# A graph kernel of three edge passes: order of the preamble's steps, and a maximum taken first in the edge pass

## What is computed

```python
def _gat(x, src, dst, W, att_src, att_dst, bias, n):
    xw = (x @ W).reshape(n, H, D)
    a_src = jnp.einsum('nhc,hc->nh', xw, att_src)
    a_dst = jnp.einsum('nhc,hc->nh', xw, att_dst)
    logits = jax.nn.leaky_relu(a_src[src] + a_dst[dst], NEG_SLOPE)
    m = jax.ops.segment_max(logits, dst, num_segments=n)
    ex = jnp.exp(logits - m[dst])
    s = jax.ops.segment_sum(ex, dst, num_segments=n)
    out = jax.ops.segment_sum(xw[src] * (ex / (s[dst] + EPS))[..., None], dst, num_segments=n)
    return out.mean(axis=1) + bias

h = relu(_gat(x, ..., W1, ...) + (x @ lW1 + lb1))
y = layernorm(x + _gat(h, ..., W2, ...) + (h @ lW2 + lb2))

ef = jnp.concatenate([y[src], y[dst]], axis=-1)
att = relu(ef @ W_lin.T + b_lin)
mx = segment_max(att, dst); ex = jnp.exp(att - mx[dst]); den = segment_sum(ex, dst)
new = segment_sum(ex / den[dst] * ef, dst)
out = layernorm(y + new @ W_out.T + b_out)
```

## Time and profile before

| | us |
|---|---|
| median of 3 runs | 6001.7 |
| lowest, highest | 5996.33, 6004.03 |
| profiled execution | 6000.85 |
| its span, first to last instruction | 5999.0 |
| busy: PE, DVE, ACT, POOL | 3932.5, 3794.1, 3054.0, 4434.3 |
| PE's granted clock, mean | 0.602 |
| first pass gathers, from and to | 14.59 to 1986.9 |
| second pass gathers | 2013.71 to 3965.2 |
| edge pass gathers | 4000.67 to 5951.5 |

### The profile page before, as it was taken

How to read it: one execution, slowest core, us unless ns; L and a number is a source line. 1 busy time by engine, 2 the same in 40 slices (tenths; PEclk the granted TensorE clock), 3 DMA queues, 4 the chain that set the end, 5 groups by cost and what they waited for, 6 DMA issues and landing times. The chain is left out here.

```text
span 5999.0 us, 87084 instructions
## 1 busy us (share of the span) xinstructions
PE 3932.5 (66%) x21980; PEld 3616.2 (60%) x21980; DVE 3794.1 (63%) x9640; ACT 3054.0 (51%) x5829; POOL 4434.3 (74%) x4701
## 2 busy tenths in 40 slices
PE   6655555555555466666666666657777777777776
PEld 5555555555555455555555555547777777777776
DVE  5544444444444555555555555559999999999998
ACT  3333333333333355555555555546666666666666
POOL 6777777777777677777777777757777777777775
PEclk7666665666666556565656565655556555565565
DMA  7322222222222222222222222223333333333332
GB/s 163 70 63 63 63 63 63 63 63 63 63 63 63 54 67 66 66 66 66 66 66 66 66 66 66 66 62 90 89 90 90 89 89 89 89 90 90 90 89 59
DMA packets 354105, 444.77 MB, mean 74 GB/s; under 512 B 142144, under 2 KB 233658, under 8 KB 353444
## 3 DMA queue, kind: packets, MB, share of 16 engines
q0 software_dynamic: 150112, 217.86, 17.1%
q10 hardware_dynamic: 50400, 132.89, 6.8%
q1 hardware_dynamic: 153508, 93.04, 6.0%
HBM read 407.88 MB, written 39.55 MB: 75 GB/s over the span
## 5 line engine op out<-in xcount | busy, mean ns | idle before, releaser
L1044 POOL DMA_INDIRECT rows<-tab,idx_now x4653 | 4392.2, 944 | 1495.1 <-issue 1416.8
L2015 PE MATMUL psum<-share,rows 128*65 128x132 f32 (+10 forms) x6240 | 1177.0, 381 | 0.0
L1288 DVE TENSOR_TENSOR_SCAN psum<-cut,psum 48x224 f32<-48x224 bf16 (+3 forms) x524 | 450.4, 882 | 1087.7 <-PE psum L1988 1071.3
L2015 PEld LDWEIGHTS psum<-share,rows 128*65 128x65 f32 x6240 | 1093.3, 224 | 5.4
L2105 PE MATMUL psum<-own,hot_t 112*128 112x64 f32 x3126 | 666.2, 408 | 385.8 <-DVE mix L1497 354.5
L1988 PE MATMUL psum<-ident,strip 128*48 128x128 f32 (+1 forms) x786 | 208.8, 402 | 1071.3 <-ACT strip L1686 1070.7
L2105 PEld LDWEIGHTS psum<-own,hot_t 112*128 112x128 f32 x3126 | 644.4, 317 | 411.1 <-DVE near L1558 224.1
L1988 PEld LDWEIGHTS psum<-ident,strip 128*48 128x48 f32 (+1 forms) x786 | 82.6, 133 | 1156.7 <-issue 1143.8
L2121 PE MATMUL psum<-hot,prob 128*128 128x112 f32 x3126 | 665.1, 406 | 1.4 <-DVE prob L1589 1.4
L2121 PEld LDWEIGHTS psum<-hot,prob 128*128 128x128 f32 x3126 | 645.8, 317 | 1.6 <-DVE prob L1589 1.6
L1664 ACT ACTIVATE hot_t<-away,ones 112x1536 bf16<-112x1536 f32 (+2 forms) x393 | 616.2, 1568 | 12.8
(11 more groups left out here) (239 smaller groups left out, 5739.5 us busy)
## 6 DMA issues: line engine op xcount, KB each, us to landing
rel_t<-rel_row ACTq DMA_DIRECT2D x256, 336.0 KB
rows<-tab,idx_now POOLq DMA_INDIRECT x4653, 2.5
rel_t<-rel_runs ACTq DMA_DIRECT2D x128, 336.0 KB
own<-tab SPq DMA_DIRECT2D x262, 63.0 KB
cut<-cut_row SPq DMA_DIRECT2D x130, 120.2 KB
tab<-row SPq DMA_DIRECT2D x131, 112.0 KB
tab<-row SPq DMA_DIRECT2D x131, 63.0 KB
own<-tab SPq DMA_DIRECT2D x131, 56.0 KB
```

The costliest lines, as they stand in the source:

```text
L1044: nc.gpsimd.indirect_dma_start(rows_of[p][:, G * c.s + j, 0:D] if raw else rows_of[p][:, G * c.s + j, :], None, x if raw else halves[p], b ...
L1288: done = nc.vector.tensor_tensor_scan(running, cuts[:, 0:-1], values, NEG, ALU.add, ALU.max)
L2015: done = nc.tensor.matmul(summed[:, :, LO[j]:HI[j]], rows_g[:, at + j, 0:D + 1], of[:, j, :, 0:SUBS[j]], start=not opened, stop=j == chunk ...
```

## The change

It has three parts.

1. **Indices of the first units.** The first 36 chunks of src are loaded by a transfer of their own at the head of SP's queue (36 partitions of 128). DVE casts them after its first two memsets, PE transposes them once, DVE copies them to idx_now. ACT's three copies are gone.
2. **First table.** The loads of dst, its tail and the first part of x stand ahead of SP's first wait. DVE makes the weights' products ahead of the steps on dst, and the 19 groups go between these steps: 0 to 3 after the casts, 4 to 7 after rel_f and prev_f, 8 to 11 after rel_b, 12 to 15 after cut_b, 16 to 18 after rel_all. SP's stores are placed likewise: 0 ahead of the later weights, 1 among them, 2 after rel_row, 3 ahead of spread_cuts(0), 4 behind it. PE's transposes of rel_f come after the product of group 13. end_i is loaded behind copy_dst in the first pass, and end_at is made by DVE ahead of the last four units of that pass.
3. **Edge pass.** The table holds -Pd instead of Pd. near = max(-Pd, Ps) is taken first, and the scans and transposes run on near; the segment's maximum goes back into PSUM (middle), and logit3 = near - middle. With relu(Pd + Ps) = max(Ps, -Pd) + Pd the own part drops out of the difference. over, back, DVE's step on over and ACT's relu are gone.

The core of the diff (of a block of steps that moves as a whole, the first or last line stands):

```diff
+        src0_i, src0_f = rel_f[0:G * RAW, 0:P].bitcast(I32), dst_f[0:G * RAW, 0:P]
...
+            sp.dma_start(src0_i, src[0:RAW * UE].rearrange("(p e) -> p e", e=P)).then_inc(src0_in, 16)
             sp.dma_start(src_i[:, :], src[0:P * UE].rearrange("(p e) -> p e", p=P)).then_inc(src_in, 16)
...
+            sp.dma_start(dst_i[0:1, P:DW], dst[0:DW - P].rearrange("(p e) -> p e", p=1)).then_inc(dst_in, 16)
+            for q0, q1 in ((1, 113), (113, P)):
+                sp.dma_start(dst_i[q0:q1, :], bass.AP(dst.tensor, q0 * UE - P, [[UE, q1 - q0], [1, DW]])).then_inc(dst_in, 16)
+            sp.dma_start(dstl_i[:, :], dst[FULL * UE:E].rearrange("(p e) -> p e", p=1)).then_inc(dst_in, 16)
+            x_rows = x[0:XP * (XB - 1), :].rearrange("(p b) c -> p (b c)", p=XP)
+
+            def load_x(k):
+                e0, e1 = XPARTS[k]
+                sp.dma_start(x_in_sb[:, e0 * D:e1 * D], x_rows[:, e0 * D:e1 * D]).then_inc(x_moved[min(k, len(XLOADED) - 1)], 16)
+
+            load_x(0)
             sp.wait_ge(cleared, 1)
             sp.dma_start(srct_i[0:2, :], src[P * UE:FULL * UE].rearrange("(p e) -> p e", p=2)).then_inc(src_in, 16)
             sp.dma_start(srct_i[2:3, 0:LAST], src[FULL * UE:E].rearrange("(p e) -> p e", p=1)).then_inc(src_in, 16)
...
-            sp.dma_start(dst_i[0:1, P:DW], dst[0:DW - P].rearrange("(p e) -> p e", p=1)).then_inc(dst_in, 16)
...
             sp.wait_ge(cleared, 2)
...
-            sp.dma_start(dstl_i[:, :], dst[FULL * UE:E].rearrange("(p e) -> p e", p=1)).then_inc(dst_in, 16)
...
-            for k, (e0, e1) in enumerate(XPARTS):
-                sp.dma_start(x_in_sb[:, e0 * D:e1 * D], x_rows[:, e0 * D:e1 * D]).then_inc(x_moved[min(k, len(XLOADED) - 1)], 16)
+            for k in range(1, len(XPARTS)):
+                load_x(k)
             sp.wait_ge(cleared, 4)
...
-            sp.dma_start(end_i[:, :], bass.AP(dst.tensor, (FULL - 1) * UE, [[0, P], [UE, 2]])).then_inc(base_in, 16)
...
+            def store_x(k):
+                e0, e1 = XPARTS[k]
+                done = len([g for g in XGROUPS if g[0] < e1])
+                sp.wait_ge(coef_kept, 2 * done)
+                sp.wait_ge(x_kept, done)
+                half = k % 2 * XPART
+                sp.dma_start(tab_rows[:, e0:e1, :], x_tab[:, half:half + e1 - e0, :]).then_inc(x_moved[min(k, len(XLOADED) - 1)], 16)
+
+            store_x(0)
             sp.dma_start(w_in[1][:, :], W2).then_inc(weights_in, 16)
...
+            store_x(1)
...
             sp.wait_ge(rel_made, 2)
             sp.dma_start(rel_row[0:P * UE].rearrange("(p e) -> p e", p=P), rel_b[:, :]).then_inc(rel_out, 16)
             sp.dma_start(rel_row[P * UE:EP].rearrange("(p e) -> p e", p=LASTC), relt_b[:, :]).then_inc(rel_out, 16)
+            store_x(2)
             sp.wait_ge(rel_made, 4)
...
+            store_x(3)
             sp.wait_ge(cut_out, 64)
             spread_cuts(0)
+            store_x(4)
+            e0, e1 = XPARTS[4]
+            sp.dma_start(tab[0][XP * (XB - 1):N, :], x_tab[0:XREST, XB - 1 - e0, :]).then_inc(x_moved[-1], 16)
...
+            sp.wait_ge(base_in, 20)
...
                         copy_dst()
+                        sp.dma_start(end_i[:, :], bass.AP(dst.tensor, (FULL - 1) * UE, [[0, P], [UE, 2]])).then_inc(end_in, 16)
...
+            dve.wait_ge(src0_in, 16)
+            nc.vector.tensor_copy(src0_f, src0_i).then_inc(src_cast, 1)
             nc.vector.memset(srct_i[:, :], 0).then_inc(cleared, 1)
+            dve.wait_ge(src_turned, 1)
+            nc.vector.tensor_copy(idx_now[:, 0:RAW, :].rearrange("p s j -> p (s j)"), bank_c[:, 0:G * RAW])\
+                .then_inc(idx_staged, RAW)
...
-            dve.wait_ge(dst_in, 96)
...
-            nc.vector.tensor_copy(prev_all[:, :], bank_h[:, 128:128 + NU]).then_inc(rel_kept, 1)
...
+            def table_rows(g0, g1):
+                for g, (e0, e1) in list(enumerate(XGROUPS))[g0:g1]:
...
+            dve.wait_ge(dst_in, 96)
...
+            table_rows(0, 4)
+            nc.vector.tensor_scalar(rel_f[:, :], dst_f[:, P:P + UE], base_f[:, 0:1], None, ALU.subtract)\
...
+            table_rows(4, 8)
+            nc.vector.tensor_scalar(rel_b[:, :], dst_f[:, P:P + UE], base_f[:, 0:1], None, ALU.subtract)\
...
+            table_rows(8, 12)
+            dve.wait_ge(src_turned, 5)
+            nc.vector.tensor_tensor(step_f[:, :], dst_f[:, P:P + UE], dst_f[:, P - 1:P + UE - 1], ALU.subtract)\
...
+            nc.vector.tensor_scalar(cutt_b[:, :], stept_f[:, :], NEG, None, ALU.mult).then_inc(rel_made, 1)
+            table_rows(12, 16)
+            dve.wait_ge(base_in, 16)
...
+            nc.vector.tensor_copy(prev_all[:, :], bank_h[:, 128:128 + NU]).then_inc(rel_kept, 1)
+            table_rows(16, NXG)
...
+                if p == 0:
+                    dve.wait_ge(end_in, 16)
+                    nc.vector.tensor_copy(end_f[:, :], end_i[:, :]).then_inc(prep_step, 1)
+                    dve.wait_ge(prep_step, 64)
+                    nc.vector.tensor_scalar(end_at[:, :], end_f[:, :], row_no[:, 0:1], None, ALU.add).then_inc(end_ready, 1)
...
+                dve.wait_ge(own3_ready, c.u + 1)
+                if not c.below(2):
+                    dve.wait_ge(out_made, c.u - 1)
+                nc.vector.tensor_tensor(near[:, 0:m, :], added3[:, 0:m, :], rows_e[:, at:at + m, D:2 * D], ALU.max)\
+                    .then_inc(near_ready, 1)
+                dve.wait_ge(near_ready, c.u + 1)
                 dve.wait_ge(beside_kept, c.u + 1)
                 nc.vector.transpose(turned_e.rearrange("p (j e) -> p j e", j=2)[:, :, HALO:HALO + run_len]
                                     .rearrange("p j (c b) -> p c j b", b=QUAD),
-                                    rows_e[:, at:at + m, D:2 * D].rearrange("p c (j a) -> p c j a", a=QUAD))\
+                                    near[:, 0:m, :].rearrange("p c (j a) -> p c j a", a=QUAD))\
                     .then_inc(body_turned, 1)
...
-                nc.vector.transpose(back[:, 0:m, :].rearrange("p c (j a) -> p c j a", a=QUAD),
+                nc.vector.transpose(middle[:, 0:m, :].rearrange("p c (j a) -> p c j a", a=QUAD),
...
-            def with_own(c):
-
-                at, m = G * c.s, chunks(c)
-                dve.wait_ge(own3_ready, c.u + 1)
-                if not c.below(2):
-                    dve.wait_ge(out_made, c.u - 1)
+            def logits3(c):
+
+                m = chunks(c)
                 dve.wait_ge(back_ready, c.u + 1)
-                nc.vector.tensor_tensor(over[:, 0:m, :], added3[:, 0:m, :], back[:, 0:m, :], ALU.add).then_inc(added_ready, 1)
-                nc.vector.tensor_tensor(near[:, 0:m, :], added3[:, 0:m, :], rows_e[:, at:at + m, D:2 * D], ALU.add)\
-                    .then_inc(near_ready, 1)
+                if not c.below(1):
+                    dve.wait_ge(prob_kept, c.u)
+                nc.vector.tensor_tensor(logit3[:, 0:m, :], near[:, 0:m, :], middle[:, 0:m, :], ALU.subtract)\
+                    .then_inc(logit_ready, 1)
...
             for c in units(dve):
                 n, k, m = NU * p + c.u, c.k, chunks(c)
-                dve.wait_ge(over_ready, c.u + 1)
-                dve.wait_ge(near_ready, c.u + 1)
-                nc.vector.scalar_tensor_tensor(out=logit3[:, 0:m, :], in0=near[:, 0:m, :], scalar=0.0, in1=middle[:, 0:m, :],
-                                               op0=ALU.max, op1=ALU.subtract).then_inc(logit_ready, 1)
...
                     last_most(c.plus(1))
-                    with_own(c.plus(1))
+                    logits3(c.plus(1))
...
-                act.wait_ge(src_turned, k + 1)
-                nc.scalar.activation(idx_now[:, 0:RAW, 4 * k:4 * k + 4].rearrange("p s j -> p j s"),
-                                     bank_e[:, 512 * k:512 * k + 512].rearrange("p (j u) -> p j u", j=4)[:, :, 0:RAW], ACT.Copy)\
-                    .then_inc(idx_staged, 1)
...
-                    nc.scalar.activation(row3[c.k][:, 0:D], extra[:, D:2 * D], ACT.Copy).then_inc(row_kept_a, 1)
+                    nc.scalar.activation(row3[c.k][:, 0:D], extra[:, D:2 * D], ACT.Copy, scale=-1.0).then_inc(row_kept_a, 1)
...
-            def relu_over(c):
-                act.wait_ge(added_ready, 2 * NU + c.u + 1)
-                m = chunks(c)
-                nc.scalar.activation(middle[:, 0:m, :], over[:, 0:m, :], ACT.Relu).then_inc(over_ready, 1)
...
+            pe.wait_ge(src_cast, 1)
+            nc.tensor.transpose(bank_c[:, 0:G * RAW], src0_f, ident[0:G * RAW, 0:G * RAW]).then_inc(src_turned, 1)
+            pe.wait_ge(src_cast, 3)
...
+            def turn_rel():
+                pe.wait_ge(prep_step, 61)
...
+                if g == 13:
+                    turn_rel()
```

156 lines of the change are left out of this document (65 added, 91 removed).

## The result

The changed kernel takes 5991.6 us (median of 20 runs, 5987.4 to 6002.7), the kernel before 6000.8 in runs beside it (20, 5995.8 to 6006.5). The ratio is 0.9985, with a 95% interval of 0.9979 to 0.9992. So 9.2 us go, 0.15%, of the 13.8 that the forecast of 5987 would take from 6000.8: less than the 0.2% that the forecast calls a difference. The profiled execution is the longest of the 20, 6002.7 us with 6000.9 of span, and has to be read stretch by stretch.

What follows compares the result with a forecast made beforehand. The prediction took POOL's gathers to bound the kernel, with gains only before and behind them: 10.3 (first table) + 4.1 (end) = 14.4 us off, median 5987.3, stated as 5987; 8-in-10 range 5979 to 5994.

Steps and rivals of the forecast that it cites:

- Gathers bound the kernel: All passes: POOL starts a gather every 1.248 us, 4689 of them making 5852 us of the 5999.
- rival E: Edge pass: DVE bounds it after all, so 124 us faster, 5877; chance 0.01.
- First indices: Preamble: first gather near 6 (range 5 to 11) instead of 14.59; gives nothing by itself unless the table is ready.
- First table, 10.3 us: First table: reordered DVE steps end its last group at 57.6 against 67.94, 10.3 us off.
- the weights' products wait for lW1 until 16: First table's walk: DVE's weights' products (2.9 us) wait for the lW1 load until 16 and end at 18.9.
- By the same 10.3: Unit 6 of pass 1: its chain starts at DVE's last table row, so it moves from 125.86 to 115.6.
- The slow raw gathers: Preamble: 9 raw gathers at 2.17 us until 25.44, then 27 at 1.248; they end near 59 instead of 64.5.
- The end, 4.1 us: Behind the last gather: fewer DVE steps and no ACT relu in the last units take about 4.1 us off.
- Edge loop 14.5 under 14.98: Edge pass: DVE's loop takes 14.5 us a unit, under POOL's 14.98, so DVE waits for the gathers.
- The 0.7 us of wait for own rows: Edge pass, each unit: DVE waits 0.7 us for own rows and last_mix ahead of the scans.
- Rival B: First table: TensorE slow, all groups 1.93 us apart, 4 us of the gain gone, 5991; chance 0.26.
- Rival D: Edge pass: DVE's new wait for own rows exceeds 0.7 us; at a 15.3 loop the kernel takes 6029; chance 0.04.

Runs made afterwards that it cites:

- e12: Kernel before with parts 1 and 2 of the change and 6 of the 12 own-row products made twice: 5998.8 us, ratio 0.9999.
- e6: Changed kernel with SP issuing parts 1 to 4 of x only after the first layer's eight weight loads landed: 8161.5 us against 7806.7 before, ratio 1.0451.
- e1: The changed kernel run again, unaltered: 8154.3 us against 7803.4 for the kernel before beside it, ratio 1.0453.
- e3: Changed kernel with the edge pass of the kernel before, so parts 1 and 2 alone: 7794.9 us against 7803.4 before, ratio 0.9989.
- e11: Kernel before with 6 of the 12 own-row products of each edge-pass unit made twice: 7732.4 us against 7752.6 before, ratio 0.9976.
- e9: Changed kernel with TensorE's own rows a unit earlier and the last product in its own bank: 8094.6 us against 7752.6 before, ratio 1.0445.

## Why the forecast was right or wrong

The time was right, 5987 for 5991.6, inside 5979 to 5994, and the mechanism in the main too: POOL sets the pace, and time comes off in front of and behind its gathers alone. The direction was not the likeliest one: the forecast had 0.67 on faster by over 0.2%, and it was 0.15%. A third of the gain is missing, 4.6 us of 13.8, which a time of 6000 hides; and of the forecast's signs of being wrong one came, a last table row later than 62 (62.03, ending at 62.56). The first gather of the table (69.13 for 62 to 67) and the wait at unit 6 (6.8 for some 5) lie outside too. DVE's share "down to about 93%" was misread: 92.9% is the share before, and it went to 87.8%.

- **Gathers bound the kernel**: right where TensorE does not pause. DVE's share fell by 5 points, POOL kept its pace, nothing of rival E's 124 us came.
- **First indices**: right, 5.43 for 6. No row had the landing of the small load; it was issued at 0.72 and the copy that follows let POOL start at 5.43. Worth nothing by itself, as POOL then waits 13.4 us for the table.
- **First table, 10.3 us**: the step that failed. 4.8 came at unit 6 in the first profile, 6.2 in e12. The term "the weights' products wait for lW1 until 16" measured 23.58, the start of the products. The 16 fits the kernel before, where the two loads of lW1, issued by 5, took 9.7 and 11.6 us to land; in the changed one they took 15.5 and 18.7. The walk moved loads of dst and x ahead, and kept the landing of a small transfer that shares the engines with them; e6, which holds 2.5 MB of x back, has the products at 15.89. That put the first group 7.3 us late; 2.3 came back by the last one, as turn_rel took 2.6 us and not 4.7.
- **"By the same 10.3" at unit 6**: the mechanism was right and the size not. The last row of the table came 5.4 us earlier, and 0.6 of it was lost on the way to unit 6.
- **The slow raw gathers**: the forecast went by the loads and had them end at 59; they ended at 55.7. The rows of POOL above and of DVE tell why. The gather at 14.39 took 1.84 us beside the cast at 14.29, the one at 48.46 took 2.46 beside step_f; between 16.5 and 23, with the loads still running and DVE idle, each took 0.95. Not every overlap costs: the gather at 69.13 starts together with such a step of DVE (L1237) and takes 0.95 too, the next one 1.36. The Trainium skill (SBUF — State Buffer, section SBUF: two separate sides) has it so: engines and DMA don't contend, and a DVE step that takes the shared port holds GpSimd off. The trace agrees in the rows named first, and the reading by the loads falls.
- **The end, 4.1 us**: right, 4.7, read in one profile of each kernel.
- **Edge loop 14.5 under 14.98**: right in that DVE waits for the gathers, 1.17 us a unit. The 0.7 us of wait for own rows was not seen, as DVE waited for the gathers just before; it shows in e1.
- **Rival B** came in small part: two steps from group to group of 1.9 and 2.0 us (30.61 to 32.51, 43.38 to 45.38), 1.0 to 1.5 in the others that waited for TensorE without other steps between. They cost some 2 us, and not the 4 of all groups at 1.93.
- **Rival D, 0.04**: in the first measurement it did not decide. Where TensorE pauses, its wait is the whole result. That the first measurement had no pauses is luck for the forecast: in e1 the same kernel takes 2167 us more than 5987, of which 1803 are in the kernel before as well. The rival's price had been drawn from one profile, in which own rows take 5.35 us each time; nothing in it showed how long they can take. The forecast saw the wait and what is queued behind it, and did not ask what work the old order had kept for that wait.

## What to carry to other kernels

Where a wait moves ahead of work that needed nothing from its releaser, that work was the cover for every delay of the releaser. Price the move by a late releaser too, not only by the one duration that a profile shows: 0.7 us a unit by the profile, and 7.3 us more at each pause, are here the step from 0.15% faster to 4.5% slower. And when a walk along a timeline moves steps, the landings of transfers don't stay: count the bytes issued beside a small transfer. Parts 1 and 2 with the old edge pass look like the safe choice: 0.9989 with pauses (e3), and the last gather 5.9 us earlier without (e12). By themselves they were not run without pauses.

## What the runs showed of the hardware

- The kernel before took 7753 us and, later on the same chip, 6001, each time steady within 0.2%. With the pauses TensorE's matmuls stand 0.7 to 2.9 us apart for some 15 us at a time, about once in two units of the edge pass. In passes 1 and 2 DVE waited 249 times, in 262 units, for 2240.6 us in all (share_prev, e1). In pass 1 the matmuls don't even stand apart there: those of one unit are recorded until 636.4, and ScalarE and DVE, which wait for them, start at 644.21 and 644.31.
- With pauses, 2.7 us more work a unit on TensorE took 20 us less time (e11, 7732.4 for 7752.6).
- In a pause DVE's transposes and scans run at their usual durations, 0.99, 2.21 and 2.00 us, and the gathers at 0.94.
- Own rows recorded as run in 2.80 us released the step that waits for them 30 us after their start (e9).
